# Euler stage in powers of L^3, with its pieces in one pause of each reflection

## What is computed

```
# layer 0, h = relu(layernorm(x)), 8 Euler steps with dt = 1/8
h0 = h @ fc_in_w.T + fc_in_b
alph = sigmoid(alpha);  w_eff = (w * clip(d, 0, 1)) @ w.T
h  <- h + dt * (alph*0.5*(adj @ h - h) + h @ w_eff - h + x0)     # 8 times
x  = x + h
# layer 1: eigenvectors U of the normalized Laplacian of adj
_, U = eigh(L_norm)
x  = x + U @ (relu((U.T @ h) @ W1 + b1) @ W2 + b2)
# layers 2 and 3: a graph convolution with batch norms, and four small LSTMs over windows
```

## Time and profile before

| | |
|---|---|
| median of 3 runs | 4553.45 us (4543.36 to 4556.3) |
| profiled execution | 4556.2 us |
| its span, first to last instruction | 4554.4 us |
| mean granted TensorE clock | 0.795 |
| PE busy / DVE / ACT / POOL | 3184.7 / 2974.5 / 1019.2 / 780.0 us |

### The profile page before, as it was taken

One profiled execution on the slowest core, in us unless ns is written; L12 is line 12 of the kernel. 1 busy time (PEld: TensorE's weight loads), 2 busy tenths in 40 slices (PEclk: granted clock), 3 DMA queues, 4 the chain that ended last, 5 costly groups with the idle time before them and its releaser, 6 DMA issues.

```text
span 4554.4 us, 72277 instructions
## 1 busy us (share of the span) xinstructions
PE 3184.7 (70%) x22012; PEld 2163.8 (48%) x22012; DVE 2974.5 (65%) x18157; ACT 1019.2 (22%) x3735; POOL 780.0 (17%) x3360
## 2 busy tenths in 40 slices
PE   2999998998999999999400100000549584999998
PEld 1788877886887788655200000000426332444433
DVE  6687877888888888688878899999321223003323
ACT  0222222222222322222100000000031213116532
POOL 1122222222222222233222211111000000000000
PEclk7699996997998898599655555555779796889998
DMA  2000000000000000000000000000000000000000
GB/s 93 2 2 2 2 2 2 2 2 2 2 2 2 2 2 2 1 2 2 1 0 1 0 0 0 0 0 0 0 0 0 19 0 0 0 0 0 0 0 37
DMA packets 3104, 21.16 MB, mean 5 GB/s; under 512 B 432, under 2 KB 560, under 8 KB 1072
## 3 DMA queue, kind: packets, MB, share of 16 engines
q1 hardware_dynamic: 2736, 16.85, 0.9%
HBM read 12.66 MB, written 4.19 MB: 4 GB/s over the span
## 4 chain that ended last, share of the span: by engine, by line
PE 54%; DVE 33%; issue 5%; ACT 4%; POOL 3%; DMA 0%; DVEq 0%; SPq 0%; POOLq 0%; ACTq 0%
PE ps L621 7%; PE ps L951 6%; PE ps L664 6%; DVE H L1794 5%; PE ps L656 3%; PE ps L668 2%; PE ps L958 2%; PE ps L615 2%; PE ps L673 2%; PE ps L676 2%; DVE H L1383 2%; PE ps L524 2%; PE ps L923 2%; ACT H L1138 2%; PE ps L910 2%
## 5 line engine op out<-in xcount | busy, mean ns | idle before, releaser
L664 PE MATMUL ps<-C 128*32 128x131 f32 (+39 forms) x10200 | 394.9, 288 | 3.0 <-DVE C L1613 3.0
L1012 POOL TENSOR_SCALAR step<-XYEG,PQ 128x8 f32<-128x8 f32 (+3 forms) x510 | 157.9, 310 | 1236.2 <-DVE PQ L1546 1236.2
L1219 ACT ACTIVATE sz<-C,PQ 128x4 f32<-128x4 f32 (+3 forms) x510 | 151.6, 297 | 762.6 <-POOL C L1013 762.5
L621 PE MATMUL ps<-WK,LT 128*128 128x256 f32 x1024 | 307.6, 415 | 0.0
L621 PE MATMUL ps<-C,LT 128*128 128x256 f32 x1024 | 296.4, 405 | 0.0
L951 PE MATMUL ps<-C,V 128*128 128x512 f32 (+1 forms) x504 | 287.5, 727 | 8.5 <-issue 7.5
L664 PEld LDWEIGHTS ps<-C 128*32 128x32 f32 x10200 | 265.6, 118 | 39.8 <-DVE C L1613 14.5
L673 PEld LDWEIGHTS ps<-dots,ones 128*128 128x128 f32 x1020 | 177.2, 211 | 223.2 <-DVE dots L1383 145.9
L1203 ACT ACTIVATE tsc<-tsc 128x1 f32<-128x1 f32 x510 | 103.4, 203 | 768.6 <-DVE tsc L1507 768.6
L1383 DVE CUSTOM_DVE_ANT_0 jq<-SO,ps,C 128x10 f32<-128x10 f32 (+14 forms) x1199 | 220.1, 228 | 74.0 <-PE ps L686 25.0
L673 PE MATMUL ps<-dots,ones 128*128 128x2 f32 x1020 | 203.8, 270 | 60.7 <-DVE dots L1383 56.4
(11 more groups left out here) (484 smaller groups left out, 7613.2 us busy)
## 6 DMA issues: line engine op xcount, KB each, us to landing
out_x<-X SPq DMA_DIRECT2D x4, 1024.0 KB, 3.9
X<-in_x SPq DMA_DIRECT2D x2, 1280.0 KB, 20.6
X<-in_x SPq DMA_DIRECT2D x1, 1536.0 KB, 17.0
eye<-in_eye SPq DMA_DIRECT2D x1, 1026.0 KB, 9.4
WK<-in_adj SPq DMA_DIRECT2D x1, 1024.0 KB, 4.8
adjT<-in_adjT SPq DMA_DIRECT2D x1, 1024.0 KB, 6.9
WK<-in_below SPq DMA_DIRECT2D x1, 1024.0 KB, 11.0
V<-in_wih SPq DMA_DIRECT2D x1, 1024.0 KB, 4.9
```

The costliest lines, as they stand in the source:

```text
L621: m = mm(some, LT[:, mb, j * P:(j + 1) * P], state(k + 1)[:, 2 * half:2 * half + 2, mb, :], start=False, stop=(part == last), skip_group_c ...
L664: m = mm(ps[q * QUAD:(q + 1) * QUAD, 0, 0:c + n], SI[:, b, 0, 2 * j:2 * j + 1].broadcast_to([P, QUAD]), AS[:, b, q, k * QUAD:P + n], start ...
L1012: step(g_.tensor_scalar(step2[:, k:KB, :], this[:, :, 2:4], PQ[:, r % 2, 1:2], None, ALU.mult))
```

## The change

It uses three powers at a time: with y0 = x0, y1 = L x0 and y2 = L² x0, stage s (2, 1, 0) adds the three terms y0 G_3s, y1 G_3s+1 and y2 G_3s+2 to L³ times the state of stage s + 1. L, L² and L³ are formed once by 12 set-up tiles. L is then applied four times for a group (y1, y2, and L³ twice) in place of eight. The pieces go into the first pause alone, (3, 0); the last quarter's room becomes (2, 0). The filler of the third quarter grows from 256 to 384 columns. POOL's negated mask goes; the signs are moved into a -1 matrix for the dots and into three VectorE instructions. POOL writes the identity into QT in four turns behind `EULER_END`, since QT holds L and y1 until then.

```diff
-IDLE = (256, 256, 256, 384)
+IDLE = (256, 256, 384, 384)
 BANKS = 3
-ROOM = ((2, 2), (2, 2), (2, 2), (1, 1))
+ROOM = ((3, 0), (3, 0), (3, 0), (2, 0))
...
-TILES = 8 + 4 * EULER
+POWERS = 3
+SETUP = 12
+TILES = 4 * POWERS + 4 * (EULER + 1) // POWERS
+ALL_TILES = SETUP + 4 * TILES
...
+    if t < SETUP:
+        return None, ("L", "L2", "L3")[t // 4], t % 4, t
+    g, r = divmod(t - SETUP, TILES)
+    if r < 4 * POWERS:
+        return g, ("x0", "y1", "y2")[r // 4], r % 4, r
+    return g, ("s2", "s1", "s0")[(r - 4 * POWERS) // 4], r % 4, r
...
+        if kind == "L":
+            parts = [free] * 2
+        elif kind == "L2":
+            parts = tiles(0)
+        elif kind == "L3":
+            parts = tiles(4)
+        elif kind == "x0":
             if j == 0:
                 for h in range(8):
                     first = p.at(("input", 8 * g + h), first) + 1
+            parts = [free + [("input", 8 * g + 2 * j + 1)]] * 2
+        elif kind in ("y1", "y2"):
+            parts = [free + [("input", 8 * g + 2 * j + 1)]] * (2 * KB)
         else:
+            parts = [free + [("tile", base + 4 * y + 2 * half + 1)] for y in range(POWERS) for half in range(2)]
+            if kind != "s2":
+                parts += tiles(t - j - 4)
+            if kind == "s0":
+                parts += [[w]] * 2
+        i, r = p.unit(("tile", t), [free + n for n in parts], i)
+        if kind == "y2" and j == 3:
+            first = r + 1
+        if kind == "s0":
+            p.pool[r + 1].append(t)
...
+                elif kind in ("L2", "L3", "y1", "y2"):
+                    last = 2 * KB - 1
...
+                    turned = LM[:, step_, j * P:(j + 1) * P] if kind in ("L2", "L3") else B0[:, j, step_, :]
+                    m = mm(some, turned, (LT if kind in ("L2", "y1") else L2)[:, step_, 2 * half * D:2 * (half + 1) * D],
+                           start=(part == 0), stop=(part == last), skip_group_check=True)
...
-                    pe.wait_ge(S["eu_sb"], 4 * TILES)
+                    pe.wait_ge(S["eu_sb"], ALL_TILES)
                     keep_clock(idle)
...
-                mm(ps[:, 3, 0:2], ones[:], dots[:], start=True, stop=True).then_inc(S["dots_ps"], 1)
+                mm(ps[:, 3, 0:2], minus, dots[:], start=True, stop=True).then_inc(S["dots_ps"], 1)
...
-            g_.tensor_scalar(above, below, -1.0, None, ALU.mult).then_inc(S["above_ready"], 1)
...
-                g_.tensor_tensor(xm[:, k:KB].unsqueeze(2), SI[:, k:KB, 0, 2 * j:2 * j + 1], above[:, k:KB, r:r + 1], ALU.mult)\
+                g_.tensor_tensor(xm[:, k:KB].unsqueeze(2), SI[:, k:KB, 0, 2 * j:2 * j + 1], below[:, k:KB, r:r + 1], ALU.mult)\
                     .then_inc(S["xm_ready"], 1)
...
+                if EULER_END < r <= EULER_END + KB:
+                    identity(r - EULER_END - 1)
                 pool.wait_ge(S["g_ready"], r)
...
+            def identity(b):
+
+                pool.wait_ge(S["eu_sb"], ALL_TILES)
+                step(g_.memset(QT[:, b, :], 0.0))
+                g_.tensor_copy(QT[:, b, b * P:(b + 1) * P], ident).then_inc(S["qt_zero"], 1)
...
+            go(v.memset(minus, -1.0))
...
-                m_tz = ch.mark(stt(tz, mu, g1, y1, ALU.mult, ALU.subtract))
+                m_tz = ch.mark(stt(tz, mu, g1, y1, ALU.mult, ALU.add))
...
-                m_uz = ch.mark(stt(uz, tz, mu, uy, ALU.mult, ALU.subtract))
+                m_uz = ch.mark(stt(uz, tz, mu, uy, ALU.mult, ALU.add))
```

## The result

The changed kernel takes 4496.36 us (median of 4 runs: 4468.62, 4494.72, 4498.01, 4502.37) where the kernel before, on the same chip, takes 4550.9 (4 runs, 4543.36 to 4556.3): a ratio of 0.9871, 95% interval 0.9848 to 0.9894. It is 55 us faster, where 152 were forecast, and 4496 lies above the range. The profiled execution is the one of 4494.72 us.

A forecast was written before the change was run, and what follows sets the result against it. TensorE was taken as the bound of the reduction's full turns, second-pause pieces delaying the next row. Terms summed to -152 us from the profiled 4556.2, giving 4404, or 4402 as median; range 4360 to 4480.

The forecast's parts named there:

- All three between pivot element and dots: Turns 33 to 335: three pieces in the first pause put dots 0.24, 0.38 and 0.36 us later by quarter.
- What is late next is the vector x: After dots, x sets the next row at 1.14 us (1.20 third quarter); quarters 2 and 3 gain 27 and 15 us.
- turns 336 to 384: Third quarter without pieces, two 384-column fillers: 0.24 us gained a turn, -12 us, needing the high clock.
- rival 2: Tail after dots does not shrink, POOL's uz or a wait keeping 1.73 us; 68 us go: 4470; chance 0.12.
- The first quarter: Turns 33 to 112: 0.33 us gained a turn, less 5 us for the `w` pieces, -21 us.
- rival 3: Turns 336 to 416: fillers fail, clock stays low, 49 turns pay about 1.4 us more: 4529; chance 0.07.
- the start: Before the turns: POOL no longer forms the negated mask, freeing VectorE's products, -3 us.
- the empty places at the changes of group: Around turns 113, 205 and 300: empty places in the pauses vanish, -11, -12 and -16 us.
- turns 385 to 416: Start of the last quarter: turns become like the ninth row's, 4.31 to 2.95 us each, -44 us.
- Turns 1 to 32: First turns: the table's pieces go into one pause, first tile done at turn 27 instead of 18, +10 us.
- Rival 1: Full turns: thinner TensorE work lowers the clock, 2 us a turn; 4704 over half of turns 33 to 335; chance 0.09.
- Rival 4: At the group changes: dips are not the empty places' doing, so their 39 us stay: 4441; chance 0.10.

The follow-up runs named there:

- experiments 2 to 4: Two added VectorE copies a turn in the changed kernel, 4556.75 us; its diagonal copy moved to ScalarE, 4475.76; the two added copies in the kernel before, 4587.41.
- experiment 12: The changed kernel without fillers in the third quarter: 4486.54 us, ratio 0.9857 to the kernel before.
- experiment 1: The changed kernel with the new pieces in the old places, both pauses, (2, 2) and (1, 1) in the last quarter: 4517.74 us, ratio 0.9913 to the kernel before.
- experiment 9: The changed kernel with each POOL addition into X cut into quarters on four turns: 4473.65 us, ratio 0.9829 to the kernel before.
- experiment 3: The changed kernel with VectorE's copy of the diagonal element moved to ScalarE: 4475.76 us, ratio 0.9833 to the kernel before.

## Why the prediction was wrong, point by point

**The step that failed first** is in "All three between pivot element and dots": "What is late next is the vector x", and from it 0.21 and 0.19 us a turn. The working read the distance from dots to the next row and took an earlier row for an earlier turn. Norm to norm says otherwise: the norm waits for VectorE's own queue, entered by way of POOL and ScalarE, before and after (3.71 us in both; experiments 2 to 4). The 27 and 15 us of quarters 2 and 3 were nothing, and so was the 0.24 a turn of turns 336 to 384 (undisturbed panel 57.21 and 57.54). The distances themselves were partly right: from the pivot element to dots it is 1.67 us in the first quarter, as forecast, and from dots to the row 1.16, 1.40 and 1.42 us in the three quarters (medians of turns 33 to 112, 129 to 192 and 257 to 320), where 1.14, 1.14 and 1.20 stood. In the second and third g waits for POOL's uz, which rival 2 named (1.48 us in the turn shown, 872.08 to 873.56). But even a row at 1.14 would have gained nothing. The busy share misled: PE at 98 to 100% in these rows was taken for the bound, while its pieces filled the time in which VectorE worked.

**The first quarter** held in kind: 0.27 us came of 0.33 in the shortest turns, 0.20 in the median one. Of turns 33 to 112 only 5.9 of 21 us remained: the second row's clock is 0.96 where it was 0.99. Turns 59 and 60, at the low level and with pieces of y1 on the path, took 3.9 us more than before, and turn 47, the end of a panel and partly at the low level, 2.7 more. The waits of the new pieces, put at 0, are not to blame: in turns 33 to 400 no piece of the powers or the states has PE idle for over 0.1 us ahead of it. What the sum had no term for is short low stretches within full turns.

**Turns 336 to 384** went rival 3's way, in part: turns 336 to 350 at the low level took 5.0 to 5.2 us each with their two fillers. Rival 3 had them "pay about 1.4 more"; they measured 1.6. The profiled run has 25 us of it. One run, at 4468.62, is 26 us under it, which is the size of the stretch. Its mean granted clock is 0.818 where the profiled run's is 0.811, which fits a run without it; it has no trace, so that is not shown.

**Right** were the start (the four products of VectorE now take 0.68 us each, the mask being gone), the empty places at the changes of group (-20.9 for -16, -11.9 for -12 and -16.9 for -16) and turns 385 to 416 (-42.5 for -44). The middle two agree in part by luck: two and three of the additions, some 1 us each, now lie outside these rows, where the forecast had them stay. The third row of before holds one addition, not two: the one before it ended at 666.34. The products at the start:

```profile
33.32 0.68 DVE L1431 CUSTOM_DVE_ANT_0 LT<-WK,eye 128x512 f32<-128x512 f32 x1
...
35.15 0.68 DVE L1431 CUSTOM_DVE_ANT_0 LT<-WK,eye 128x512 f32<-128x512 f32 x1
```

That the two engines take turns is seen only in part there: the fourth product before (38.25) also lay within POOL's record, which ends at 39.53, and took 0.68. At an addition it is plain: both records take 1.27 us from 735.77 on.

Turns 1 to 32 gained 6.5 where +10 stood; their parts were not looked at further. Rival 1, the clock falling because full turns are thinner, came only in stretches of a few turns: the rows of full turns stand at 0.95 to 1.00, though PE is busy for 88 to 92% of them. Rival 4 fell with the empty places. An addition still costs its turn 1.0 to 1.4 us in nine of the sixteen cases, as taken; in the other seven the turn has at most 0.6 us of excess.

## What to carry to other kernels

Before an edit is priced by the distance between two operations of one engine, measure the loop from a point of each engine to the same point one turn on, and ask who reads the result and what stands ahead of it in the reader's queue. A result that comes earlier is worth only what its reader waits for it; a copy or two added to the reader's queue tells in one run whether that queue is on the path. Fillers that are to keep a clock up have to be tried where the work runs out, wider and earlier as well as not at all, since at the low level they are themselves the path. Where a low stretch comes and goes between runs, compare kernels by stage and not by their medians alone.

## What was not expected of the hardware

- The low level costs this loop little by itself: 0.2 us of 3.67 in the third quarter with nothing but its own matmuls (experiment 12, median of turns 352 to 382; 3.47 at 1.00). The pieces and fillers at half rate are what it costs.
- Two 384-column fillers held 1.00 through the fourth quarter's turns of 2.95 us. In the third's of 3.45 they held it in turns 352 to 384 of the kernel after and lost it in turn 322 of experiment 1 and turn 344 of experiment 9; 512 and 384 lost it in none of five profiles. In the kernel after the level came back only with turn 351, the last of a panel.
- The low stretches are sensitive to small shifts: with a 0.06 us shorter turn (experiment 3, one profile) the one at turns 58 to 60 is gone, that at 333 to 351 ends at 335, and that at 264 to 268 has grown to 260 to 269.
